# One ring of six PSUM banks for scores, pieces, output and projected tiles, with new slots for the steps of a causal attention block

## What is computed

```python
x = L0_attn_x                         # 8 x 1024 x 512
xn = _layernorm(x)
# attention block on xn:
xn2 = (xn - mu) * rsqrt(var + 1e-5) * norm_g + norm_b
q = xn2 @ Wq;  k, v = split(xn @ Wkv)            # 16 heads of 64
k, v = concat([null_k, k]), concat([null_v, v])  # 2 null columns
q, k = l2norm(q) * q_scale, l2norm(k) * k_scale
sim = 8 * q @ k.T - slope[h] * |j - i|           # causal
out = softmax(sim) @ v @ Wout
```

## Time and profile before

| | |
|---|---|
| time, median of 3 runs | 2700.93 us (2698.88 to 2702.91) |
| profiled execution, span from first to last instruction | 2696.2 us |
| around the span, median less span | 4.7 us |
| PE busy | 2622.8 us, 97% |
| DVE busy | 2488.1 us, 92% |
| ACT busy | 2126.7 us, 79% |
| POOL busy | 2098.1 us, 78% |
| mean granted TensorE clock | 0.993 |

### The profile page before, as it was taken

The page is one execution under the profiler, slowest core; times in us unless marked ns, Lnnn a source line. Parts: engine busy times, 40 slices in busy tenths (PEclk is TensorE's granted clock), DMA queues, the critical chain, the costliest instruction groups (busy, mean ns, idle before and its releaser), DMA issues.

```text
span 2696.2 us, 84329 instructions
## 1 busy us (share of the span) xinstructions
PE 2622.8 (97%) x31631; PEld 1575.9 (58%) x31631; DVE 2488.1 (92%) x6760; ACT 2126.7 (79%) x3385; POOL 2098.1 (78%) x2438
## 2 busy tenths in 40 slices
PE   5799999999999999999999999999999999999997
PEld 4455565565565565565555565565655665565654
DVE  8999998999999999999999999999998999989986
ACT  5688887888877888877887878787887888877876
POOL 6677887779867788678887788777887778877775
PEclk8899999999999999999999999999999999999999
DMA  5333344434544334333443435433353433544222
GB/s 177 67 63 74 81 102 99 91 71 82 102 100 94 69 87 98 96 87 76 90 107 82 93 75 101 100 95 71 80 107 87 100 74 76 98 100 80 54 59 71
DMA packets 638790, 236.94 MB, mean 88 GB/s; under 512 B 594609, under 2 KB 596657, under 8 KB 638385
## 3 DMA queue, kind: packets, MB, share of 16 engines
q1 hardware_dynamic: 636912, 231.45, 39.6%
q10 hardware_dynamic: 1472, 0.09, 0.0%
HBM read 72.01 MB, written 16.78 MB: 33 GB/s over the span
## 4 chain that ended last, share of the span: by engine, by line
PE 81%; DVE 7%; issue 3%; DMA 2%; POOL 1%; SPq 1%; ACT 1%; DVEq 0%; POOLq 0%; ACTq 0%
PE PS L1259 12%; PE PS L1236 11%; PE PS L1238 10%; PE PS L1237 10%; PE PS L1283 6%; PE PS L1322 6%; PE PS L1326 4%; PE PS L1324 4%; PE PS L1263 4%; PE PS L1349 4%; PE PS L1350 3%; PE PS L1351 3%; DVE PS L1034 3%; DVE AR L1075 1%; PE PS L1294 1%
## 5 line engine op out<-in xcount | busy, mean ns | idle before, releaser
L1034 DVE CUSTOM_DVE_ANT_0 PS<-PS,STR 128x512 f32<-128x512 f32 (+3 forms) x1536 | 822.5, 580 | 121.9 <-PE PS L1283 114.9
L598 ACT ACTIVATE AR<-PS,SC 128x1024 f32<-128x1024 f32 (+1 forms) x640 | 655.1, 1024 | 143.5 <-PE PS L1294 75.7
L1236 PE MATMUL PS<-WH,XT 128*128 128x388 f16 x2048 | 676.7, 330 | 22.5 <-DVE AR L1047 13.5
L1237 PE MATMUL PS<-WL,XT 128*128 128x388 f16 x2048 | 673.9, 329 | 0.0
L1238 PE MATMUL PS<-WH,XT 128*128 128x388 f16 x2048 | 673.7, 329 | 0.0
L602 ACT ACTIVATE AR<-AR 128x1024 f16<-128x1024 f32 (+1 forms) x640 | 622.0, 972 | 20.3
L803 POOL TENSOR_TENSOR RN<-SS,HALF 128x8 f32<-128x8 f32 x256 | 453.6, 1772 | 182.7 <-DVE SS L1122 181.6
L1075 DVE TENSOR_TENSOR AR<-AR 128x768 f16<-128x768 f32 (+1 forms) x448 | 503.4, 1134 | 11.8 <-ACT AR L602 11.7
L1259 PE MATMUL PS<-AR 64*128 64x512 f16 (+3 forms) x4608 | 495.4, 324 | 9.1 <-ACT AR L598 8.9
L1322 PE MATMUL PS<-AR 128*128 128x66 f16 x4608 | 472.3, 195 | 1.8 <-DVE AR L1075 0.8
L1324 PE MATMUL PS<-AR 128*128 128x64 f16 x4608 | 468.8, 192 | 0.0
(11 more groups left out here) (227 smaller groups left out, 5197.2 us busy)
## 6 DMA issues: line engine op xcount, KB each, us to landing
XW<-in_L_attn_x SPq DMA_DIRECT2D x112, 256.0 KB, 3.0
XB<-in_L_attn_x SPq DMA_DIRECT2D x64, 256.0 KB, 3.0
out<-ACC SPq DMA_DIRECT2D x64, 256.0 KB, 2.3
ACC<-in_L_attn_x SPq DMA_DIRECT2D x56, 256.0 KB, 3.0
AR<-QKB SPq DMA_TRANSPOSE x512, 2.5
AR<-in_L_attn_Wkv SPq DMA_DIRECT2D x2, 1536.0 KB, 12.7
ACC<-in_L_attn_x SPq DMA_DIRECT2D x2, 1024.0 KB, 7.1
AR<-in_L_attn_Wout SPq DMA_DIRECT2D x1, 2048.0 KB, 8.4
```

What stands on the lines that cost most here:

```text
L598: e.activation(PR[:, n % 2, :, 0:wide], SB[:, :, 0:wide], ACT.Exp, scale=SIG).then_inc(s_p, 1)
L1034: e.tensor_tensor_reduce(out=r[:, 0:n], in0=r[:, 0:n], in1=ST[:, u % 2, h, o:o + n], scale=1.0, scalar=LOW, op0=ALU.add, op1=ALU.max, accu ...
L1236: e.matmul(to, XT[:, k, xs], WH[:, k, p, :], start=k == 0, stop=False)
L1237: e.matmul(to, XT[:, k, xs], WL[:, k, p, :], start=False, stop=False)
```

## The change

Scores leave their two banks and join the ring, which now has banks 0 to 5 (`BANKS = 6`); `AV` moves to banks 6 and 7. `take_pair` gives both heads of a score step two neighbouring banks, and `bank_free` has a fourth case: a bank that held scores is free when the exponential is done (s_p). The two short first pieces are put behind one another in one bank: (0, 0) with (2, 0), and (4, 1) with (6, 1), which leaves ten groups of pieces; VectorE still reduces each piece by itself, after the whole group. Within a slot, pieces now come ahead of scores. ScalarE's cast has slots of its own (`W_CAST`). The value step no longer waits for s_nv2. In the opening the four small additions to VNT (L1137) move from VectorE to GpSimd, two XW steps move behind the DG step, and the steps for Wout's maximum are due earlier. All slot tables are new, and SL is 50.

```diff
-BANKS = 4
-SL = 48
+BANKS = 6
+SL = 50
...
-PIECES = [(qt, c) for qt in range(NT) for c in range(1 + qt // 4)]
+GROUPS = [[(0, 0), (2, 0)], [(3, 0)], [(1, 0)], [(4, 0)], [(5, 0)], [(4, 1), (6, 1)], [(6, 0)], [(5, 1)], [(7, 0)], [(7, 1)]]
...
-W_SCORE = [88, 96, 105, 108, 111, 115, 118, 126, 130, 133]
...
+W_SCORE = [98, 99, 112, 113, 115, 115, 119, 128, 140, 141]
+W_CAST = [100, 107, 114, 114, 115, 115, 127, 128, 142, 144]
...
-HOLD = [2.0, 2.1, 2.0, 6.7]
...
+HOLD = [9.6, 10.3, 10.7, 13.0, 10.4]
...
+    def take_pair(slot, u, m):
+        i = min(range(BANKS - 1), key=lambda z: (max(read[z], read[z + 1]), read[z] + read[z + 1]))
+        for h in range(2):
+            who = ("sc", u, 2 * m + h)
+            at[who], before[who] = i + h, last[i + h]
+            last[i + h], read[i + h] = who, slot
...
-        SB, AV = PS[:, 0:2, :], PS[:, 2:4, 0:264]
+        AV = PS[:, 6:8, 0:264]
...
-            return PS[:, 4 + BANK[who], :]
+            return PS[:, BANK[who], :]
...
-                e.wait_ge(s_mx, 24 * u + i + 1)
+                e.wait_ge(s_mx, 24 * u + pieces(i // 2)[-1][4] + i % 2 + 1)
+            elif what == "sc":
+                e.wait_ge(s_p, NS * u + i // 2 + 1)
...
-                    e.activation(PR[:, n % 2, :, 0:wide], SB[:, :, 0:wide], ACT.Exp, scale=SIG).then_inc(s_p, 1)
+                    e.activation(PR[:, n % 2, :, 0:wide], PS[:, low:low + 2, 0:wide], ACT.Exp, scale=SIG).then_inc(s_p, 1)
+                for u, m in due(s, W_CAST):
...
+            w.wait_ge(s_grp, 1)
+            for q in range(4):
+                ins = e.tensor_scalar(VNF[:, :, q, 64], VNF[:, :, q, 64], MSK[:, 8 + q:9 + q], None, ALU.add)
...
-                    n = NS * u + m
-                    w.wait_ge(s_p, n)
+                    low = BANK["sc", u, 2 * m]
+                    bank_free(w, "sc", u, 2 * m)
+                    bank_free(w, "sc", u, 2 * m + 1)
...
-                    if blocks[0][0] == 0:
-                        w.wait_ge(s_nv2, 2 * u + qc + 1)
```

More of the change, by code:

```diff
@@ L63 @@
[L63 to L81, removed]
@@ L96 @@
[L96 to L113 removed]
+W_PIECE = [51, 51, 64, 68, 79, 86, 86, 88, 92, 94]
@@ new lines @@
+W_KV = [9, 12, 16, 18, 29, 37, 40, 48]
+W_VL = [9, 11, 24, 24, 29, 35, 36, 54]
+W_STRIP = [32, 34]
+W_SQ = [12, 24, 40, 53]
+W_SS = [15, 24, 36, 59]
+W_POW = [19, 29, 54, 68]
+W_TP = [26, 34, 51, 56]
+W_HI = [25, 37, 60, 65]
+W_LO = [28, 35, 60, 70]
+W_ROWS = [64, 77]
+W_SHIFT = [69, 103]
+W_CTP = [76, 98]
+W_NX = [84, 100]
+W_NL = [83, 117]
+W_NTT = [90, 102]
+W_XA = [-379, -338, -316, -260, -236, -211, -195, -180]
+W_STAT = [-337, -270, -238, -234, -212, -197, -177, -146]
+W_XB = [-173, -128, -80, -64, -38, -18, -16, 24]
@@ L116, in due, with pieces @@
+def pieces(g):
+    out, at = [], 0
+    done = 2 * sum(len(z) for z in GROUPS[:g])
+    for qt, c in GROUPS[g]:
+        n = min(512, P * (qt + 1) - 512 * c)
+        out.append((qt, c, at, n, done))
+        at += n
+        done += 2
+    return out
 def due(slot, when, units=NU, period=SL):
@@ L155, in ring_order @@
             take(s + HOLD[1], "s", u, 2 * i + 1)
+        for u, m in due(s, W_SCORE):
+            take_pair(s + HOLD[4], u, m)
         for u, t in due_op(s, W_OP):
@@ L1242, in _ @@
             for s in SLOTS:
+                for _, i in due(s, W_WOT, 1, BL):
+                    if i == 0:
+                        w.wait_ge(s_wo, 1)
+                        e.transpose(PS[0:1, 6, 0:P], AM[:, 5:6], IDF[:, :]).then_inc(s_won, 1)
+                    else:
+                        w.wait_ge(s_wop, 1)
+                        e.matmul(PS[:, 6, P:P + 1], ONE[0:1, :], M8[0:1, :], start=True, stop=True).then_inc(s_won, 1)
+                for u, i in due(s, W_PIECE):
+                    bank_free(w, "s", u, 2 * i)
+                    bank_free(w, "s", u, 2 * i + 1)
+                    for qt, c, at, n, done in pieces(i):
+                        for g in range(qt // 2 + 1):
+                            w.wait_ge(s_kq[g], 32 * (u + 1))
+                        for h in range(2):
+                            hs = slice(64 * h, 64 * h + 64)
+                            e.matmul(rb("s", u, 2 * i + h)[:, at:at + n], KQ[hs, u % 2, QH, P * qt:P * qt + P],
+                                     KQ[hs, u % 2, KH, 512 * c:512 * c + n], start=not at, stop=True,
+                                     skip_group_check=True).then_inc(s_s, 1)
                 for u, m in due(s, W_SCORE):
                     qc, blocks = STEPS[m]
-                    n = NS * u + m
-                    w.wait_ge(s_p, n)
+                    low = BANK["sc", u, 2 * m]
+                    bank_free(w, "sc", u, 2 * m)
+                    bank_free(w, "sc", u, 2 * m + 1)
                     for g in range(max(2 * qc + 1, blocks[-1][0] // 2) + 1):
```

133 lines of the change are left out of this document (69 added, 64 removed).

## The result

The change takes 2710.0 us (median; 2707.87 to 2713.15), the kernel before 2700.93 us: ratio 1.0036, interval 1.0025 to 1.0048. It is slower, by 9.1 us. The forecast was 2692; the range ended at 2709, one us short. Run once more on another chip (experiment 5) it took 2707.37 against 2699.13 us, ratio 1.0029 (1.0017 to 1.0040).

The account below looks back on a forecast made before the run. TensorE was taken to bound the middle and VectorE the opening; -0.7 (matmul places) - 7 (ring) + 2 (opening) - 3 (tail) = -8.7 us from 2700.93 us gave 2692 us, range 2680 to 2709.

Parts of the forecast that it names:

- signs named beforehand: Opening: VectorE idle near 6 us, first tile at 77; middle: waits 3 us, not 10; end: exponential under 4 us.
- Places where 64-row and 128-row matmuls meet: On TensorE, such places fall from 1283 to 1276 at 0.1 us each: -0.7 us.
- The ring in the middle: Between 150 and 2600 us, most TensorE waits for banks lose their cause: -7 us, bounds -10 and 0.
- The opening: Up to 150 us, earlier Wout steps delay TensorE 8.7 us, but VectorE sets the pace: +2 us, bounds +8.7 and -3.
- The tail: From 2600 us, four output tiles cover the last exponential, cast and subtraction: -3 us, bounds -7.4 and +3.9.
- The cast: On ScalarE, its own slot releases a score bank up to 1.06 us earlier: part of the -7 us.
- The wait for s_nv2: On TensorE, the dropped wait was already met by TensorE's own order: no gain.
- Slots that keep VectorE and GpSimd apart: If slots really part the two engines, all 10 us go and the sum is 2689; the forecast stayed with -7.
- The output weights hold TensorE: Rival: the opening's 8.7 us stand in full and the middle gives nothing: 2709 us, chance 0.12.
- the middle gives nothing: Second half of the 2709 us rival: no gain in the middle, where the forecast took -7 us.
- The transpose queue: Rival: loads of x ahead of the keys' transposes make keys late in seven later batches: 2713 us, chance 0.06.
- the clock in the middle: Rival: new waits make TensorE fall to half clock once in each of eight batches: 2712 us, chance 0.02.

Follow-up runs that it names:

- experiment 5: The change itself, unaltered, run again beside the kernel before on another chip: 2707.37 us, ratio 1.0029.
- experiment 2: The change with GpSimd's first two statistics steps for the next batch two slots earlier and VectorE's last reading for them four earlier: 2691.88 us, ratio 0.9977.
- experiment 9: The kernel before with the second step of the null values moved behind the piece of 128 columns (slot 115 to 116): 2729.85 us, ratio 1.0118.
- Experiment 7: The kernel before with only the steps for Wout's maximum moved early, as in the change: 2706.98 us, ratio 1.0028.
- experiment 1: The change with only the steps of Wout put late again: 2700.52 us, ratio 1.0012.
- experiment 4: The change with ScalarE's cast back in the slot of its exponential: 2798.6 us, ratio 1.0375.

## Why the prediction was wrong

The forecast was -8.7 us, the result +9.1. Of the signs named beforehand those of the opening came (VectorE idle 5.30 us ahead of the maximum, first tile at 77.44 us, TensorE's wait 20.66 us behind two tiles), and so did the one of the end (2.8 us for the exponential). The one of the middle did not: 23 us of waits and not 3. Term by term:

*Places where 64-row and 128-row matmuls meet, -0.7.* Nothing contradicts it; it is too small to be seen alone.

*The ring in the middle, -7.* Measured +1.5 and -1.9 us over six batches. The step that failed is "What is late next is not VectorE's throughput, which has 27 us of slack in 400, but its order": what was late was the order on GpSimd, which I had not followed at all. I counted how much TensorE work stands between two tenants of a bank and held it against readers that are in time; `W_SMALL` moved with all the other tables, and I gave it no cost and named no cover for it. Moving its first two steps by two slots gave 14 to 16 us (experiment 2). So the middle's zero is two things that happen to cancel. With the statistics out of the way a batch is 2.4 us shorter than before: 14.6 us over the six that were measured, 19 over eight by the same rate, an estimate. I had 7, so the gain from ring and slots was there and larger than I took it. No run shows how it divides between the ring, the new order and the wait for s_nv2 that was dropped. Part of the reason for the size may be that I summed the view of waits (10 us) and missed the 9.9 us of experiment 9, which it does not show.

*The opening, +2, bounds -3 and +8.7.* Measured +7.4 and +7.6 to the ninth unit, +7.6 and +7.8 to the third: the working was right to a few tenths (maximum ends at 75.5 for 75.2, first tile 77.44 for 77.3), and the choice inside the bounds was wrong. The step that failed is "It is not the value, because VectorE sets the pace here and loses less". Being busy 46.58 of 50 us in the kernel before was no proof of that: VectorE stood 5.30 us for the load, then 4.2 us for tiles that TensorE and ScalarE brought late, and was busy 38.03 us. Experiment 7 shows the price with nothing else changed, +7.9; experiment 1 takes 5 to 7 us back.

*The tail, -3.* Measured +0.6 and +4.1; the six other profiles with the new slots of the units and six banks, experiment 4 left out, have +2.0 to +4.4. The exponential's 7.4 us fell to 2.8 as expected, but low halves (3.7 us), row maxima (2.7) and the transposes of the outputs (3.1, where it was 1.8) took their place. The granted clock fell too, behind a stretch from 2675 to 2680 us in which TensorE was busy 3.43 of 5 us. The row of 2680 to 2690 us, after and before:

```profile
2680.00:2690.00 10.00, 8.40 (x91) 5.10 (x88) 2.73 (x3) 6.57 (x8) 6.24 (x5) 0.83 0.19 54
```

```profile
2680.00:2690.00 10.00, 7.64 (x100) 4.35 (x94) 4.57 (x6) 2.58 (x4) 1.88 (x2) 1.00 0.26 80
```

The step that failed is "I take -3 us, as those tiles cover the last exponential, cast and subtraction": the end did not get shorter in any of these profiles. No run isolates this part, so its cause stays open.

*The cast, part of the -7.* The direction was right and the size far off: without its own slots the change is at 2798.6 us (experiment 4).

*The wait for s_nv2, nothing.* True in the kernel before, where a piece or a projected tile always stood between. In the change the null values are followed straight by a value step in half of the units (the starts are 0.21 us apart there, with no wait); with the wait kept they would be 0.44 apart, as in experiment 9: 0.23 us in each of 32 units, about 7 us. That is an estimate; no run puts the wait back.

*Slots that keep VectorE and GpSimd apart.* By the means they don't. The low halves of 768 columns on VectorE, in the groups by line and shape, before and after:

```profile
L1075 DVE TENSOR_TENSOR AR<-AR 128x768 f16<-128x768 f32 x256 | 254.9, 1014 | 6.3 <-ACT AR L602 6.2
```

```profile
L1112 DVE TENSOR_TENSOR AR<-AR 128x768 f16<-128x768 f32 x256 | 249.5, 995 | 27.2 <-ACT AR L630 27.2
```

The means are 1014 and 995 ns, and 1294 and 1296 for the shape of 1024 columns. By the Trainium skill's rule (page "SBUF — State Buffer", section "Who interferes with whom") a VectorE instruction with two SBUF inputs contends with a GpSimd instruction that reads SBUF. The single case, 2.06 against 0.95 us, agrees in kind: beside the slow one GpSimd ran two instructions of 512 columns (L863, L871), beside the fast one only one of 8 columns (L803). The 10 us that the prediction worked out by that rule had parted slots as their condition, and with means as close as these the slots did not part the two.

*The rivals.* "The output weights hold TensorE", 2709 us, is what came, nearly to the us, and that is luck in part. Its first half is right: the delay of the opening stands almost in full. Its sign (VectorE pauses of over 5 us from 75.8 to 150 us) was there, 8.7 us in all, 4.2 of them for ScalarE's reads; but it was a weak sign, as the kernel before already had 6.3 us of them from 70.4 us on. Its other half, "the middle gives nothing", was a plain assumption: the middle gave nothing because the statistics on GpSimd's queue took back what the ring and the slots gave. Its sum also leaves the tail at nothing, without saying so. The transpose queue was no trouble (1.2 us of waits for keys from 150 us on, in two places), nor was the clock in the middle: 1.00 from 150 to 2600 us. The Trainium skill (page "TensorE: Matmul & The Clock Gate", section "A second HAM failure mode: psum-queue depth-cycling") tells of a kernel whose clock swung as it cycled through PSUM banks, with short idle times of TensorE between. Six banks in turn show no such swing here; with five, where TensorE was idle 12% of the time, the granted clock was 0.98.

## What to carry to other kernels

When all slots move, what is done once per batch moves too: follow it on every engine, to see what it stands behind and who waits for the next item of that queue. Here 3.3 us of GpSimd work per batch, placed behind a wait instead of ahead of it, cost 14 to 16 us in all through ScalarE and a PSUM bank. And where two engines are nearly equally busy, "the other one sets the pace" is no ground to discount a delay; take the full shift unless the trace shows slack behind it.

In this kernel the larger ring of banks was worth something only with the slots, and the slots only with the ring: 6 banks in the old slots +62 us, 5 banks in the new ones +486 us, both together with one queue mended -6 us (2691.88 against 2697.93), with the output weights late too -9.5 us (2688.47). Neither half was fitted again for the other, so the two large numbers are what an unfitted half costs, not what the best order with it would.

## What the runs showed that I had not expected

- A wait shorter than the modelled rest of the matmul in front does not appear in the view of waits. Distances between starts show it: 0.16 us, 61 times.
- A value step that waits for a semaphore which TensorE itself gives with the matmul just in front starts 0.44 us behind it, and 0.21 us behind it in the kernel without that wait: 0.23 us, though the order on TensorE is the same.
- The order of ScalarE's queue weighs heavily here: seven of a unit's ten casts, 1.06 us each, put earlier in it, three of them past an exponential, cost over 90 us over 64 units, 1.4 us in each.
